# Writing out the loop over pairs of head groups in the attention stage of a transformer block

## The reference

```python
qkv = (x @ w_qkv).reshape(B, S, 3, heads, head_dim)
Q, K, V = qkv[:, :, 0], qkv[:, :, 1], qkv[:, :, 2]
Q, K = apply_rope(Q), apply_rope(K)
attn = jnp.einsum('bqhd,bkhd->bhqk', Q, K) * scale
attn = jnp.where(causal, attn, NEG_INF)
attn = jax.nn.softmax(attn, axis=-1)
out = jnp.einsum('bhqk,bkhd->bqhd', attn, V).reshape(B, S, dim)
return out @ w_proj + b_proj
```

## Time and profile before

| | us |
|---|---|
| runs | 3441.1, 3438.6, 3434.5 |
| median | 3438.6 |
| the profiled execution | 3415.0 |
| its span (first to last instruction) | 3413.2 |

### The profile page before, as it was taken

One profiled execution on the slowest core, in us unless ns is written; L12 is line 12 of the kernel. 1 busy time (PEld: TensorE's weight loads), 2 busy tenths in 40 slices (PEclk: granted clock), 3 DMA queues, 4 the chain that ended last, 5 costly groups with the idle time before them and its releaser, 6 DMA issues. The chain is left out here.

```text
span 3413.2 us, 71032 instructions
## 1 busy us (share of the span) xinstructions
PE 2933.9 (86%) x22564; PEld 1632.4 (48%) x22564; DVE 2577.0 (76%) x4840; ACT 1558.7 (46%) x2096; POOL 879.7 (26%) x1098
## 2 busy tenths in 40 slices
PE   5885479999898999989899997883999999788888
PEld 3553123333233333323233323773888888677776
DVE  3885788889888898888898851776677777566666
ACT  1443046666666666666666674110444444211111
POOL 1775001110111110111101111566233223233333
PEclk7998579999999999999999998775999999899999
DMA  2676311211121111212111103665555445322222
GB/s 69 184 201 175 77 28 49 55 35 48 47 54 51 42 44 47 52 47 56 39 44 47 47 6 79 202 210 174 157 157 162 150 156 159 103 93 92 92 92 74
DMA packets 385921, 315.60 MB, mean 92 GB/s; under 512 B 112636, under 2 KB 372200, under 8 KB 385640
## 3 DMA queue, kind: packets, MB, share of 16 engines
q1 hardware_dynamic: 373352, 278.44, 28.6%
q0 software_dynamic: 12288, 33.57, 2.9%
HBM read 194.27 MB, written 116.92 MB: 91 GB/s over the span
## 5 line engine op out<-in xcount | busy, mean ns | idle before, releaser
L871 ACT ACTIVATE probs<-ps_s 128x1024 f32<-128x1024 f32 (+3 forms) x1280 | 1078.0, 895 | 676.1 <-PE ps_s L1030 675.6
L895 DVE TENSOR_REDUCE piece_rest<-ps_m 128x1 f32<-128x512 f32 (+3 forms) x1344 | 800.2, 647 | 107.3 <-PE ps_m L1005 48.8
L895 DVE TENSOR_REDUCE piece_late<-ps_m 128x1 f32<-128x512 f32 (+2 forms) x960 | 587.0, 667 | 66.6 <-PE ps_m L1005 35.7
L1030 PE MATMUL ps_s<-q_st,k_st 50*128 50x512 bf16 (+7 forms) x5120 | 596.3, 347 | 37.1 <-issue 17.1
L1045 PE MATMUL ps_o<-probs,vs 128*32 128x512 f32 (+3 forms) x5120 | 605.1, 545 | 11.2 <-POOL probs L851 9.9
L851 POOL TENSOR_SCALAR_AFFINE_SELECT probs<-probs 128x256 f32<-128x256 f32 x512 | 205.0, 406 | 1551.8 <-ACT probs L871 1547.7
L996 PE MATMUL ps_m<-k_st,q_st 48*128 48x512 bf16 (+3 forms) x2560 | 451.4, 366 | 163.8 <-DVE piece_rest L895 78.6
L996 PEld LDWEIGHTS ps_m<-k_st,q_st 48*128 48x128 bf16 x2560 | 114.7, 93 | 784.4 <-DVE piece_rest L895 386.8
L1030 PEld LDWEIGHTS ps_s<-q_st,k_st 50*128 50x128 bf16 (+1 forms) x5120 | 224.3, 95 | 269.0 <-ACT probs L871 97.3
L1753 ACT ACTIVATE act_g<-ps_g 128x512 f32<-128x512 f32 x117 | 70.0, 599 | 279.1 <-PE ps_u L1845 279.1
L1790 DVE TENSOR_TENSOR hid_f<-act_g,ps_u 128x512 f32<-128x512 f32 x117 | 80.5, 688 | 126.4 <-ACT act_g L1753 126.4
(11 more groups left out here) (226 smaller groups left out, 5005.9 us busy)
## 6 DMA issues: line engine op xcount, KB each, us to landing
qk_parts<-parts SPq DMA_DIRECT2D x128, 192.0 KB, 2.8
k_st<-qk_parts SPq DMA_DIRECT2D x768, 32.0 KB, 1.8
q_st<-qk_parts SPq DMA_DIRECT2D x768, 32.0 KB, 1.8
x_r<-expert_rows SPq DMA_DIRECT2D x39, 512.0 KB, 4.4
expert_made<-made SPq DMA_DIRECT2D x39, 512.0 KB, 2.9
x_in<-in_L_attn_x_dram SPq DMA_DIRECT2D x32, 512.0 KB, 5.2
v_ones<-v_out SPq DMA_DIRECT2D x64, 256.0 KB, 4.6
vs<-v_ones SPq DMA_DIRECT2D x64, 256.0 KB, 3.8
```

What stands on the lines that cost most here:

```text
L871: act.activation(probs[:, u % PSLOTS, 2 * pair:2 * pair + 2, j * P:ST], ps_s[:, pair, :, j * P:ST], ACT.Exp, scale=SCALE).then_inc(exp_don ...
L895: v.tensor_reduce(dst, ps_m[:, bank, 0:n * w].rearrange("p (n w) -> p n w", n=n), AX.X, ALU.max) \
L1030: last = pe.matmul(ps_s[:, pair, z, j * P:ST], k_st[rows, slot, half, pair, kc * P:(kc + 1) * P], q_st[rows, slot, half, pair, qt * ST + j ...
```

## The change

The five loops of the attention stage become Python loops, so that the program holds each group's instructions one after another. Nothing else is edited. The work, its order on each engine, the buffers and the number of waits by meaning are as before.

```diff
-            with sp.Fori(1, GROUPS // 2 - 1) as it:
+            for it in range(1, GROUPS // 2 - 1):
                 body(it, 0, False, True, True)
                 body(it, 1, False, True, True)
...
-            with pool.Fori(0, GROUPS) as g:
+            for g in range(GROUPS):
...
-            with act.Fori(1, GROUPS) as g:
+            for g in range(1, GROUPS):
                 body(g, False)
...
-            with v.Fori(1, GROUPS // 2 - 1) as it:
+            for it in range(1, GROUPS // 2 - 1):
                 body(it, 0, False, PLAN, True)
                 body(it, 1, False, PLAN, True)
...
-            with pe.Fori(1, GROUPS // 2 - 1) as it:
+            for it in range(1, GROUPS // 2 - 1):
                 body(it, 0, False, PLAN, NITEM, True)
                 body(it, 1, False, PLAN, NITEM, True)
```

## The result

The changed kernel takes 3397.7 us at the median of 4 runs (3395.9 to 3399.7), the kernel before, run beside it, 3436.6 (3434.1 to 3441.1): a ratio of 0.9892, 95% interval 0.9875 to 0.9908, or 38.9 us less. A second, later comparison gave 3410.6 against 3440.4, ratio 0.9909 (0.9892 to 0.9927), 29.8 us less. The forecast was 3408.3, 30.3 us less, with a range of 3397 to 3422.

What follows compares the result with a forecast made beforehand. PE, busiest at 86% of the span, and DVE were taken to bound it, handing banks back and forth; 21.6 + 0.7 + 4.5 + 1.0 + 2.5 = 30.3 us less, 3438.6 - 30.3 = 3408.3 us, range 3397 to 3422.

Steps and rivals of the forecast that it cites:

- The comparison on which it rested: Attention stage: crossings between pairs with a jump (group 4, 106.22 us) against the same without one (group 14, 101.78 us).
- The jumps with PE's and DVE's constants: Attention stage: five jumps taken, 21.6 us, plus constants replacing registers on PE and DVE, 0.7 us, gained.
- lies inside PE's stop, and goes with it: Pair crossing: DVE's late next instruction falls within PE's stop and disappears with it; included in the 21.6 us.
- rival of cheap jumps: Attention stage: stop belongs to the place, five jumps cost 0.3 us; 3429.6 us, or 3438 without constants' gain; chance 0.04.
- ACT's constants: Exponentials holding their own wait for scores: 0.32 us a group, 4.5 us in groups 1 to 14, 1.0 in group 15.
- POOL's constants: Attention stage: register instruction between POOL's wait and operation goes; 2.5 us gained, middle of 0 to 5.1.
- SP, and ACT's and POOL's jumps: Attention stage: SP's five jumps and ACT's and POOL's jumps are covered by other work; gain nothing.
- Streaming stops ACT and POOL: Rival: written-out ACT and POOL code arrives late by DMA, 60 to 120 us of stops, near 3480 us; chance 0.03.
- The stages behind: Stages after attention: price 0, bounds -6.4 to +3, as DVE's 6.41 us middle-stage delay may go or grow.
- the 23.6 us between the profiled execution and the median: Whole kernel: the runs' median stood 23.6 us above the profiled execution; carried over whole into the forecast.

Runs made afterwards that it cites:

- second profile of before: The kernel before, unchanged, profiled again: median 3433.3 us of 10 runs, ratio 0.9997, profiled execution 3434.0 us, middle stage 309.9 us instead of 289.6.
- jumps_only: Against the kernel before, only PE, DVE and SP written out, ACT and POOL keep their loops: median 3407.5 us against 3434.4, ratio 0.9921.
- no_pool: Against the kernel before, all loops written out except POOL's: median 3398.7 us, ratio 0.9896.
- pe_only: Against the kernel before, only PE's loop written out, DVE and SP still jump: median 3441.5 us, ratio 1.0003.

## Why the prediction was right or wrong

**The comparison on which it rested** held. The crossings without a jump in the trace before were what all crossings became: 101.79 us in the kernel without jumps and with registers on ACT, 101.80 and 101.78 in groups 1 and 14 of before. The jumps with PE's and DVE's constants were priced at 22.3 us and measured 22.4 against the second profile of before, 21.2 against the first.

**That DVE's jump "lies inside PE's stop, and goes with it"** was true only of the change as a whole. It read like a side effect of PE's jump; it is a second cause of the same size. A change of PE alone, priced by the same reasoning, would have been forecast at 22 us, and measured 0. The step looked at who ended last in a trace with both, which can't tell one cause from two that overlap.

**The branch's own time** was read for more than it says. The prediction took ACT's 0.045 us as the sign of a cheap jump, and DVE's and ACT's branches as the price in its rival of cheap jumps. ACT's long loop reads 0.045 us too, with a stop of 2.5 us behind it, and DVE's 0.063 us stands before one of 2.8 to 3.1. On these engines the price shows only at the next instruction. For ACT's short loop the conclusion was right all the same (0.24 us).

**ACT's constants** were mis-sized: 4.5 + 1.0 us forecast, 7.8 measured. The stage went from 1748.8 to 1740.4 us, 8.4 less, but 0.6 of that lie ahead of group 1, where ACT's program is the same in both kernels. In the last group 1.2 us were measured for 1.0 (from its first to its last position 80.13 us in `jumps_only`, 78.95 in `no_pool`). For the groups before it the measure was taken from position 15 to 39, and there it is 0.32 us again: in the kernel after, group 1 takes from 599.35 to 657.98, 58.63 us, as group 0 did in the earlier trace rows.

```profile
599.35 0.38 ACT L871 ACTIVATE probs<-ps_s 128x256 f32<-128x256 f32 x1 [0.36 <-PE ps_s L1030]
...
657.98 0.38 ACT L871 ACTIVATE probs<-ps_s 128x256 f32<-128x256 f32 x1 [2.01 <-PE ps_s L1030]
```

But a group has two more places of the same kind, one among its first positions (0.07 us) and one at the crossing (0.08), which the stretch left out. 14 x 0.47 = 6.6, not 4.5.

**POOL's constants** were taken at the middle of a range, 2.5 us, and are 0. The two errors cancel, which is luck: 8.0 us forecast for ACT and POOL together, 7.8 measured.

**SP, and ACT's and POOL's jumps** at nothing: right, at most 1 us for SP. The pages of the Trainium skill were used for the rule that a dear jump is one whose target is not held ("Runtime: NRT & Kernel Launch", "Instruction fetch mechanics"); the trace agrees, with 0.24 us for ACT's short loop, 2.5 us for its long one, and a packet of code in each long stop. The rival beside which stood the 0.108 us of the Trainium skill ("Advanced Engine Details and Errata", "Control Flow Timing") fell: the dear jumps of PE take 4.0 us.

**Streaming stops ACT and POOL** did not happen. ACT written out brought 12 more packets of code on q14 between 464 and 2000 us (37 in `jumps_only`, 49 in `no_pool`), POOL 6 more (55 in the kernel after), where 30 were estimated, and no stop. The kernel before had 89, so the packets did not stay as many: DVE's and SP's jumps had needed theirs. Written-out DVE has two hitches of 0.35 and 0.25 us in 16 groups, at the same places in every kernel that writes it out; they are in groups 7 and 11 above. That is all that the ruler shows against straight code here, and what makes these hitches is not shown.

**The stages behind** at 0 with -6.4 to +3: the delay of 6.41 us went to 3.03, and the time did not follow. The step that failed is another one: the 23.6 us between the profiled execution and the median were carried over as if they belonged to profiling. They belonged to one execution with a middle stage of 289.6 us. The forecast of the median is not hurt by it, since both cases carry it; the forecast of 3384.7 us for the profiled execution was 11.8 too low.

Attention stage: 30.3 us forecast, 29.8 to 31.0 measured. The first median's 38.9 lay near the edge of the range, the second's 29.8 at the forecast.

## What to carry to other kernels

Look for the place in the trace where the loop begins or falls through: it is the same crossing without the jump, and gives its price with all that follows from it. When several engines jump at the same point, take all their dear jumps away or none: each can hide behind the other, and a trial on one engine will say that jumps are free. A short loop (here 214 instructions, not 638) need not be written out for the sake of its jump; but ACT's was worth 7.8 us written out, for the constants in its waits.

## What the runs showed of the hardware

- A jump back of a loop of 638 instructions on ACT stopped it for 2.5 to 2.6 us, one of a loop of 214 for 0.24. Behind every long jump a packet of code starts some 1 us after the branch. The time of the branch instruction itself does not tell the two apart on ACT.
- What follows a short stop of TensorE can cost more than the stop: 2.3 us of waiting in a crossing that cost 4.9 (`pe_only`), with the clock at 1.2 GHz for 6.8 us behind it. The lower clock lasted 3.4 us in some crossings and 6.8 in others of the same program, and so a crossing cost 3.9 to 5.5 us. In the one profiled execution with ACT's and POOL's loops written out all five had the long one, though PE's stop was no longer.
- On ACT and POOL, a wait against a constant is held by the operation itself, one against a register by an instruction of the sequencer ahead of it. The exponential came 23 ns behind the scores' semaphore with a constant and 101 with a register. This was worth 0.47 us in a group of 101.8, gathered at six places; the same on POOL was worth nothing.
- Straight code on PE (15282 instructions in the whole program as built) ran through the attention stage without a stop that the ruler shows.
